# Cross-attention with an FP4 feed-forward: value products of two steps issued as one block, with three probability slots and one value buffer

## The reference

```python
def layer(x, ctx, Wq, Wk, Wv, Wo, bo, w_gate, w_up, w_down):
    t = layernorm(x)                                   # eps 1e-5
    Q, K, V = heads(t @ Wq), heads(ctx @ Wk), heads(ctx @ Wv)
    attn = softmax(einsum("bhnd,bhmd->bhnm", Q, K) * 16 ** -0.5)
    x = x + merge(einsum("bhnm,bhmd->bhnd", attn, V)) @ Wo + bo
    t = fp4(layernorm(x))                              # blocks of 16 along the width
    h = silu(t @ fp4(w_gate).T) * (t @ fp4(w_up).T)
    return x + fp4(h) @ fp4(w_down).T
```

## Time and profile before

| what | us |
|---|---|
| median of 3 runs (3525.02 to 3530.06) | 3528.58 |
| profiled execution: device time | 3532.97 |
| profiled execution: span, first to last instruction | 3531.2 |
| PE busy in the span | 3420.3 |
| DVE busy | 2947.5 |
| ACT busy | 2298.8 |
| POOL busy | 1036.9 |

### The profile page before, as it was taken

One profiled execution on the slowest core, in us unless ns is written; L12 is line 12 of the kernel. 1 busy time (PEld: TensorE's weight loads), 2 busy tenths in 40 slices (PEclk: granted clock), 3 DMA queues, 4 the chain that ended last, 5 costly groups with the idle time before them and its releaser, 6 DMA issues.

```text
span 3531.2 us, 55990 instructions
## 1 busy us (share of the span) xinstructions
PE 3420.3 (97%) x19606; PEld 1560.4 (44%) x19606; DVE 2947.5 (83%) x6697; ACT 2298.8 (65%) x4512; POOL 1036.9 (29%) x1114
## 2 busy tenths in 40 slices
PE   7899999999999999999999999999999999999996
PEld 3333444444444444444444444444444444444334
DVE  6878888888888988888888888988888888888865
ACT  2667666667666667666667666667666667666662
POOL 1323222333322333222333322333222333322222
PEclk7999999999999999999999999999999999999998
DMA  4332233232232332233232232332232232232210
GB/s 81 57 51 45 39 57 50 34 62 36 49 51 44 53 44 45 40 57 48 36 62 35 49 52 43 54 44 43 42 57 46 38 62 32 49 55 35 38 24 8
DMA packets 154263, 163.02 MB, mean 46 GB/s; under 512 B 58071, under 2 KB 127080, under 8 KB 153984
## 3 DMA queue, kind: packets, MB, share of 16 engines
q1 hardware_dynamic: 153984, 159.45, 28.6%
HBM read 46.22 MB, written 8.39 MB: 15 GB/s over the span
## 4 chain that ended last, share of the span: by engine, by line
PE 72%; DVE 23%; ACT 2%; POOL 1%; issue 1%; DMA 1%; SPq 1%; ACTq 0%; DVEq 0%
PE out_ps L912 18%; PE score_ps L901 16%; PE piece_ps L926 16%; DVE piece_max L1264 13%; PE work L865 6%; PE work L876 4%; PE work L840 3%; PE work L832 3%; ACT probs L1028 1%; PE work L856 1%; PE work L821 1%; DVE ctx_T L1134 1%; DVE ctx_T L1130 1%; PE work L850 1%; PE work L873 1%
## 5 line engine op out<-in xcount | busy, mean ns | idle before, releaser
L1028 ACT ACTIVATE probs<-score_ps 128x512 f32<-128x512 f32 (+1 forms) x3328 | 1884.0, 600 | 923.7 <-PE score_ps L901 916.0
L1264 DVE TENSOR_REDUCE piece_max<-piece_ps 128x1 f32<-128x400 f32 (+1 forms) x4096 | 2110.3, 566 | 360.6 <-PE piece_ps L926 347.8
L926 PE MATMUL piece_ps<-k_stack,q_stack 96*128 96x400 bf16 (+1 forms) x4096 | 1297.5, 339 | 40.2 <-DVE piece_max L1264 28.2
L901 PE MATMUL score_ps<-q_stack,k_stack 99*128 99x512 bf16 (+1 forms) x3328 | 1252.2, 385 | 19.6 <-DMA q_stack<-neg_rows 5.3
L912 PE MATMUL out_ps<-probs,v_ones 128*17 128x512 f32 x6656 | 877.1, 599 | 0.4
L926 PEld LDWEIGHTS piece_ps<-k_stack,q_stack 96*128 96x128 bf16 x4096 | 386.0, 98 | 801.9 <-DVE piece_max L1264 548.2
L901 PEld LDWEIGHTS score_ps<-q_stack,k_stack 99*128 99x128 bf16 (+1 forms) x3328 | 324.2, 99 | 641.7 <-ACT probs L1028 494.4
L1316 POOL TENSOR_TENSOR h<-h,h_grid 128x704 f32<-128x704 f32 (+1 forms) x68 | 111.8, 1644 | 888.4 <-DVE h_grid L1092 888.4
L865 PE MATMUL work<-wgu_T,xq_T 128*128 128x512 f32 (+1 forms) x1080 | 333.7, 425 | 0.5
L912 PEld LDWEIGHTS out_ps<-probs,v_ones 128*17 128x17 f32 x6656 | 110.3, 95 | 269.4 <-issue 218.4
L865 PEld LDWEIGHTS work<-wgu_T,xq_T 128*128 128x128 f32 x1080 | 198.1, 191 | 43.9 <-issue 3.8
(11 more groups left out here) (173 smaller groups left out, 2893.4 us busy)
## 6 DMA issues: line engine op xcount, KB each, us to landing
k_stack<-k_parts SPq DMA_DIRECT2D x256, 150.1 KB, 3.6
k_stack<-k_parts SPq DMA_DIRECT2D x256, 100.1 KB, 3.9
ctx_in<-in_ctx SPq DMA_DIRECT2D x47, 384.0 KB, 3.8
k_stack<-k_parts SPq DMA_DIRECT2D x256, 50.0 KB, 3.7
q_stack<-q_parts SPq DMA_DIRECT2D x256, 48.0 KB, 2.8
x_in<-in_x SPq DMA_DIRECT2D x16, 512.0 KB, 5.0
q_stack<-q_parts SPq DMA_DIRECT2D x256, 32.0 KB, 2.1
resid<-in_x SPq DMA_DIRECT2D x62, 128.0 KB, 2.6
```

Of the source, the lines that this page charges most:

```text
L901: pe.matmul(score_ps[0:r, n % SCORE_RING, :], k_stack[:, par, slot(g, j), m * P:m * P + r], q_stack[:, par, slot(g, j), :], start=True, st ...
L926: pe.matmul(piece_ps[:, n % PIECE_RING, 0:hi - lo], q_stack[0:SROWS, par, slot(g, j), t * P:(t + 1) * P], k_stack[0:SROWS, par, slot(g, j) ...
L1028: act.activation(probs[0:r, step % 2, j, :], score_ps[0:r, (PER_GROUP * m + j) % SCORE_RING, :], ACT.Exp, scale=SCORE_SCALE).then_inc(prob ...
L1264: dve.tensor_reduce(piece_max[:, row, c:c + 1], piece_ps[:, n % PIECE_RING, 0:piece_at[c + 1] - piece_at[c]], AX_X, ALU.max).then_inc(piec ...
```

## The change

1. The value product is issued in even steps only, for two steps at once: eight products in a row (`PV_STEPS`), in steps 2, 4, ... 12 of a group for the two steps before. The one of step 12 goes alone in step 0 of the next group. A group has six double blocks and a single one where it had thirteen single ones.
2. `probs` has three slots (`PROBS_RING`), and `exp` of a step waits for the value product three steps back.
3. `v_ones` has one buffer instead of two. The value projections of the next batch (`V_AT`) stand in its last 19 half-steps, and the last two of the seven (`v_late`) in the first half-steps of the batch that uses them. ACT's copy into the buffer waits until the tiles' old values are used (`pv_done`), and PE waits for the copy (`values_ready`).
4. All tables have new numbers. `SCORE_PLACE` has different places for even and odd steps, and pieces end a half-step earlier.

The diff, cut to its core; of the tables of half-steps and weights one row stands for all:

```diff
-    [4, 6, 6, 7, 9, 11, 16, 19, 19, 20, 22, 22, 23, 26, 29, 30, 34],
...
+    [6, 6, 6, 8, 9, 9, 14, 16, 19, 19, 24, 24, 26, 26, 31, 33, 34],
...
-OWN_AT = [8, 13, 14, 16, 18]
-PRE_AT = [26, 28, 31, 33, 37, 37, 41, 42, 46, 47, 48, 49, 59, 62, 66, 69, 71, 73, 80, 85, 94, 94]
+OWN_AT = [8, 11, 12, 15, 17]
+PRE_AT = [22, 23, 26, 33, 40, 41, 44, 46, 47, 52, 58, 60, 63, 64, 71]
+V_AT = [85, 91, 92, 97, 99, 104, 106]
 RESID_AT, BIAS_AT = 1, 4
-STACK0_AT = [15, 65]
+PV_STEPS = 2
+PROBS_RING = 3
+STACK0_AT = [12, 67]
 LN1 = 5
-HEADS_OUT_AT = 1
-MAX_AT = [22, 23]
-PIECE_FROM, PIECE_TO = 0.0, 22
+HEADS_OUT_AT = 3
+MAX_AT = [22, 24]
+PIECE_FROM, PIECE_TO = 0.0, 21
...
-SCORE_PLACE = [0.1225, 0.3125, 0.5225, 0.7625]
-PIECE_SHIFT = 0.8
+SCORE_PLACE = [0.1425, 0.3525, 0.6125, 0.7225, 0.0, 0.4525, 0.6025, 0.86]
+PIECE_SHIFT = 0.7
...
-               + [("v_proj", n) for n in range(2)] + [("q_proj", 0)] + [("k_proj", 0, c) for c in range(4)]
-               + [("v_proj", n) for n in range(2, 7)])
+               + [("q_proj", 0)] + [("k_proj", 0, c) for c in range(4)])
         for h, event in zip(PRE_AT, pre, strict=True):
             put(h, *event)
             if event[0] == "ctx_T" and event[2] == 1 and event[1] < 3:
                 put(h, "load_ctx", event[1] + 1)
+    for n, h in enumerate(V_AT):
+        if h < half * PHASES and kind != "last":
+            put(h, "v_proj", n)
+        if h >= half * PHASES and kind != "first":
+            put(h - half * PHASES, "v_late", n)
...
-                    if part == 0 and (step or kind != "first"):
-                        fill.append((4 * NQ, ("weighted", step - 1)))
+                    if part == 0 and (step or kind != "first") and m % PV_STEPS == 0:
+                        back = PV_STEPS if m else 1 + (KEY_TILES - 1) % PV_STEPS
+                        fill += [(4 * NQ, ("weighted", step - n)) for n in range(back, 0, -1)]
...
-                items = [(SCORE_PLACE[j], ("scores", g * KEY_TILES + m, j)) for j in range(PER_GROUP)]
+                total, done = sum(c for c, _ in fill) or 1, 0
+                back = sum(item[0] == "weighted" for _, item in fill)
+                items = []
+                for c, item in fill:
+                    place = (done + c / 2) / total
+                    if item[0] == "weighted":
+                        if item == ("weighted", g * KEY_TILES + m - back):
+                            pair = (done + back * c / 2) / total
+                        place = pair
+                    items.append((place, item))
+                    done += c
+                items += [(SCORE_PLACE[j + PER_GROUP * (m % PV_STEPS)], ("scores", g * KEY_TILES + m, j)) for j in range(PER_GROUP)]
                 items += [((i + PIECE_SHIFT) / (upto - n), ("piece", (g + 1) % PHASES, n + i)) for i in range(upto - n)]
-                total, done = sum(c for c, _ in fill) or 1, 0
-                for c, item in fill:
-                    items.append(((done + c / 2) / total, item))
-                    done += c
...
-        v_ones = sb("v_ones", [P, 2, KEY_TILES, HEADS, V1], F32)
-        probs = sb("probs", [P, 2, PER_GROUP, NQ], F32)
+        v_ones = sb("v_ones", [P, KEY_TILES, HEADS, V1], F32)
+        probs = sb("probs", [P, PROBS_RING, PER_GROUP, NQ], F32)
...
+        def probs_slot(batch, step):
+            return (batch * STEPS + step) % PROBS_RING
...
+            def values_ready(batch, n):
+                if V_AT[n] >= 2 * STEPS and batch:
+                    return drained("last" if batch == B - 1 else "middle", batch, ("v_late", n))
+                return drained(("start", "first", "middle")[min(batch, 2)], batch - 1, ("v_proj", n))
             def weighted(batch, g, m):
                 r, step = key_rows(m), g * KEY_TILES + m
+                if g == 0 and m % 2 == 0:
+                    pe.wait_ge(*values_ready(batch, m // 2))
                 pe.wait_ge(probs_ready, count(batch, NSCORES * PHASES, PER_GROUP * (step + 1)))
                 if m == 0:
                     if g or batch:
                         pe.wait_ge(group_taken, count(batch, PHASES, g))
                 for j in range(PER_GROUP):
-                    last = pe.matmul(out_ps[32 * j:32 * j + V1, :], v_ones[0:r, batch % 2, m, PER_GROUP * g + j, :],
-                                     probs[0:r, step % 2, j, :], start=(m == 0), stop=(m == KEY_TILES - 1))
+                    last = pe.matmul(out_ps[32 * j:32 * j + V1, :], v_ones[0:r, m, PER_GROUP * g + j, :],
+                                     probs[0:r, probs_slot(batch, step), j, :], start=(m == 0), stop=(m == KEY_TILES - 1))
                 last.then_inc(pv_done, 1)
...
+                    if kind != "start":
+                        act.wait_ge(pv_done, count(batch if name == "v_proj" else old, STEPS, (PHASES - 1) * KEY_TILES + m + n))
+                    act.copy(v_ones[0:r, m:m + n, :, 0:HEAD_DIM],
...
-                if j == 0 and (batch or step >= 2):
-                    act.wait_ge(pv_done, count(batch, STEPS, step - 1))
-                act.activation(probs[0:r, step % 2, j, :], score_ps[0:r, (PER_GROUP * m + j) % SCORE_RING, :],
+                if j == 0 and (batch or step >= PROBS_RING):
+                    act.wait_ge(pv_done, count(batch, STEPS, step + 1 - PROBS_RING))
+                act.activation(probs[0:r, probs_slot(batch, step), j, :], score_ps[0:r, (PER_GROUP * m + j) % SCORE_RING, :],
```

More of the change, by code:

```diff
@@ L174, in events @@
                 put(h, "load_ctx", event[1] + 1)
+    for n, h in enumerate(V_AT):
[3 more added lines that the diff above has]
+            put(h - half * PHASES, "v_late", n)
     return at
 ROUNDS = {"heads_T", "out_proj", "xq_T", "gate_up", "h_T", "down", "heads_out", "maxima",
-          "x_T", "ctx_T", "q_proj", "k_proj", "v_proj", "w_T", "bias"}
+          "x_T", "ctx_T", "q_proj", "k_proj", "v_proj", "v_late", "w_T", "bias"}
 class Quarter:
@@ L268, in round_parts @@
             return [4 * NQ] * 2 if name == "q_proj" else [len(n) * chunk(event[2])[1] for n in PRODUCT_PARTS]
-        if name == "v_proj":
+        if name in ("v_proj", "v_late"):
             return [len(PRODUCTS) * D] * min(2, KEY_TILES - 2 * event[1])
@@ L536, in quarter @@
                     h=h[:, t % 2, :], h_grid=h_grid[:], h_small=h_small[:], h_T=h_T[:])
-            old_probs = probs[:].rearrange("p s j q -> p (s j q)")
-            old_v = v_ones[:, B % 2].rearrange("p m h v -> p (m h v)")
+            old_probs = probs[:, 0:2].rearrange("p s j q -> p (s j q)")
+            old_v = v_ones[:].rearrange("p m h v -> p (m h v)")
             old_rest = rest[:].rearrange("p s q -> p (s q)")
@@ L833, in fill @@
                                          start=(n == 0), stop=(n == len(PRODUCTS) - 1))
-                elif name == "v_proj":
+                elif name in ("v_proj", "v_late"):
                     m, u = 2 * event[1] + part, part
@@ L993, in handle @@
                         act.wait_ge(const_ready, 7)
-                    act.copy(v_ones[0:r, nxt % 2, m:m + n, :, 0:HEAD_DIM],
+                    if kind != "start":
+                        act.wait_ge(pv_done, count(batch if name == "v_proj" else old, STEPS, (PHASES - 1) * KEY_TILES + m + n))
+                    act.copy(v_ones[0:r, m:m + n, :, 0:HEAD_DIM],
                              work[0:r, 0:n * D].rearrange("p (m h d) -> p m h d", m=n, h=HEADS)).then_inc(this_drained, 1)
```

2 lines of the change are left out of this document (1 added, 1 removed), and 22 rows, old and new, of tables (PIECE_WEIGHT, POST_AT, TAIL_AT).

## The result

| | before | after |
|---|---|---|
| median of 4 runs each, us | 3526.9 (3525.0 to 3530.1) | 3591.0 (3588.0 to 3591.8) |
| profiled execution, span, us | 3531.2 | 3588.3 |

The ratio is 1.0179 [1.0163, 1.0195]: the changed kernel is 1.8% **slower**, where 1.0% less was forecast.

The account below looks back on a forecast made before the run. PE, busy 97% of the span, was taken as the bound, DVE as a second bound within groups. 3531.2 - 81 (double blocks) + 60 (scores in a row) - 15 (pieces) = 3495, stated as 3493 us for the median; range 3443 to 3540.

Parts of the forecast that it names:

- the double block: Value products on PE: a pair takes 1.94 us and saves 0.212; 384 pairs give -81 us, 5.1 per batch.
- Rival D: Value products: the double block does not chain and saves nothing, the ends are paid all the same; 3574 us, chance 0.04.
- the ends of groups 0 to 3: Scores in a row, steps 11 and 12: waits of 0.9, 1.65, 1.6, 0.5 us; +3.9 per batch, +60 us.
- the slots: Three `probs` slots: `exp` needs the value product three steps back or a block earlier; costed at nothing.
- Pieces: Pieces waiting for DVE: the busiest window is relieved, 1 us off per batch; -15 us, both ends -24 and +26.
- rival C: Double block starves DVE or meets too dense scores and pieces; other waits grow over 1.2 us per batch; 3546, chance 0.17.
- the 19 threes of scores: Threes of scores within 0.8 us, 19 per batch (9 before), each good for up to 0.3 us; used in rival C.
- the multiplication by 15.5: Group ends: +3.9 us per batch taken for 15.5 batches, as the last group has no such end; +60 us.
- the tail: Work behind the last value product: new half-steps but the same work; 0, bounds -4 and +4 us.
- What the late projections cost: Single value buffer: ACT's copies of value tiles are covered by PE's own order; costed at nothing.

Follow-up runs that it names:

- e1: Changed kernel with single value products instead of double blocks, odd steps' score places kept: 3652.1 us, ratio 1.0348.
- e3: Changed kernel with `exp` over 256 of the 512 columns, so the output is not the reference's: 3523.6 us, one execution.
- e7: e6 with single value products in the first batch alone: 3566.2 us, ratio 1.0106.
- e6: Changed kernel with `TAIL_AT` (half-steps of the tail's work) of the kernel before: 3577.7 us, ratio 1.0144.
- e5: Kernel before with its own numbers and single value products, but three slots, one value buffer and late value projections: 3565.2 us, ratio 1.0107.
- e12: Changed kernel with single value products in the first batch and numbers looked for again, then in a longer search, against the kernel before: 3529.5 us, ratio 1.0006.

## Why the prediction was wrong

**Right:** the double block. The pair's cost (1.94 us; 1.93 measured), its chaining, and 5.1 us per batch (5.5 between e1 and after, 6.2 at equal clock). Rival D is out: by the Trainium skill's rule on weight loads (TensorE: Matmul & The Clock Gate, "The mechanism") the second step would have waited for the first to drain, and in 370 of 384 blocks it began 0.87 us behind the first's start, of a step that is 0.99 us from start to next when alone. The trace does not agree with that rule here. (The same section also names a load into a background weight buffer as one that can be pulled ahead; no run tells whether that is what happens here.) Right too: the ends of groups 0 to 3, and nothing for the slots.

**The step that failed** is that of the *Pieces*: the sum took a relief of DVE for the only effect of the new order outside the ends. I had put -1 us per batch for pieces and nothing for scores elsewhere. Measured were +0.6 for pieces and +1.7 for scores elsewhere; the ends gave +5.0, not +3.9 (the 0.8 that I had subtracted for before is 0.0 in this measure). Of the granted clock there had been no term at all: it cost 0.8, most of it as the +0.7 inside the blocks. Together some 4 us per batch more than my sum, and most of it is rival C's mechanism, "meets scores and pieces that are too dense behind it". Its condition, other waits growing by over 1.2 us, was met with 2.0 (1.7 + 0.6 - 0.3) without what the clock took. I had counted the 19 threes of scores that stand too close and had left them to a rival, although ACT was the engine that the block deprives of work for longest: 1.94 us against 1.08 in its two banks. e3 shows the part of ACT's pace: with half its `exp` a middle batch is 3.0 us shorter at the same clock.

**The second failure** is the multiplication by 15.5. The first and the last batch have another mix of work, and a middle batch's sum doesn't hold there: +9.7 and +8.5 us instead of -2.2 each. e7 shows it for the first batch, where PE waits more for DVE and ACT: the double block costs 7 us there, and up to 3.7 more are the clock (e6). For the last batch the waits for scores are 20.5 us in the trace after and 11.1 before, and the clock's mean is 0.98 instead of 1.00; that it has the same cause as the first was not tried.

**The third** is the tail: "the same work", 0 with bounds of 4 us, was +11.3, shown by e6. With the new half-steps PE waits 21.4 us for POOL in the tail, with the old ones 7.8.

**The sum.** Against 3493 us: 4.35 us x 14 = 61 in the middle batches, 23 in the first and last (+9.7 and +8.5 for -2.2 each), 11 in the tail, -2 in the lead-in, and 5 from how the median stands to the profiled execution (3 above it now, 3 below it then): 98 of 98 us. The clock's part, which lies inside these terms, is 11.5 us in the middle batches.

What the late projections cost, the prediction had at nothing, looking only at their own copies, which indeed never waited in the changed kernel. e5 gives 2.7 us per batch, on the numbers of before, and names a part of it: the value projection that I moved away in thought had kept PE from reaching the maxima before SP's queue was clear for them. My step on moved work looked at the queue that it leaves, not at who arrives sooner for it. How much of it is left at the new places wasn't measured, since that needs two value buffers beside three slots.

## What to carry to other kernels

A longer block on the bound engine is priced in two sums: what it saves there, and how long each engine beside it can go on from what is buffered (here 2 banks x 0.54 us against 1.94). Where it is longer, the steps between have to carry the rest more densely, and whether they can is decided by the placement: the same block cost 17 us per batch at one set of numbers and saved 5.5 at another. So structure and places are to be judged together, each form with numbers looked for again, confirmed on the chip (e12). A step moved away also lets everything behind it arrive sooner, at queues that are not yet clear. Stages with another mix of work (first, last, tail) need sums of their own; there a gain on PE can be a loss. And a wait of TensorE can cost more than its own length: behind the new waits the granted clock fell in half of the middle batches. So read the clock per batch before a longer product is put down to another engine.

## What was not expected of the hardware

That PE, busy 95% of the span, still has stretches at 1.2 GHz in the middle of the kernel: a double block takes 3.51 us there instead of 1.84. Also how little slack the pace of ACT has: it is busy 63% of the span, yet halving its `exp` is worth 3.9 us per middle batch in the changed kernel (3.0 at the same clock) and 0.9 in the kernel before. And a transfer became late, in e5, without being touched, because its data came 1.2 us too early for its place in SP's queue.
